# Eight subtractions of 128 columns in place of four of 256 in the edge-feature split of a graph-network kernel

## The reference, cut to what matters

```
w_ij  = silu(edge_attr_64 @ rad_w0 + rad_b0) @ rad_w1 + rad_b1
w_ij += silu(edge_attr_32 @ sph_w0 + sph_b0) @ sph_w1 + sph_b1      # 256 hidden units each
alpha = (q[receiver] * w_ij * k[sender]).sum over 16 channels of each of 8 heads / 4 * cutoff
out   = segment_sum(alpha * v[sender], receiver) / 16
```

## Time and profile before

| | us |
|---|---|
| median of 3 runs | 1711.28 (1710.13 to 1714.37) |
| span of the profiled execution | 1705.9 |
| PE busy | 1540.7 (90%) |
| DVE busy | 1368.0 (80%), 3810 instructions |
| POOL busy | 1208.1 (71%), of which L781 796.9 and L791 351.6 |
| ACT busy | 954.1 (56%) |

### The profile page before, as it was taken

How to read it: one execution, slowest core, us unless ns; L and a number is a source line. 1 busy time by engine, 2 the same in 40 slices (tenths; PEclk the granted TensorE clock), 3 DMA queues, 4 the chain that set the end, 5 groups by cost and what they waited for, 6 DMA issues and landing times.

```text
span 1705.9 us, 44927 instructions
## 1 busy us (share of the span) xinstructions
PE 1540.7 (90%) x12636; PEld 1423.3 (83%) x12636; DVE 1368.0 (80%) x3810; ACT 954.1 (56%) x1412; POOL 1208.1 (71%) x1201
## 2 busy tenths in 40 slices
PE   4389898989899876999999999999999999999995
PEld 3268787878788865999999999889999899999985
DVE  9988677777779365888888888888888888888887
ACT  3245545555565565666666655556565556555654
POOL 5577777766767327777777777777777777777772
PEclk9999999999999986999999999999999999999998
DMA  3133333333333157676666666666666666666774
GB/s 121 39 97 116 102 101 101 99 106 95 105 103 113 38 162 193 185 190 189 181 184 181 182 184 179 179 188 183 179 180 178 181 182 187 180 179 180 184 193 119
DMA packets 176696, 256.68 MB, mean 150 GB/s; under 512 B 80278, under 2 KB 91213, under 8 KB 176476
## 3 DMA queue, kind: packets, MB, share of 16 engines
q0 software_dynamic: 50240, 129.44, 28.2%
q1 hardware_dynamic: 123100, 124.61, 25.9%
q10 hardware_dynamic: 3264, 1.64, 0.3%
HBM read 232.76 MB, written 22.79 MB: 150 GB/s over the span
## 4 chain that ended last, share of the span: by engine, by line
PE 40%; POOL 30%; issue 13%; DVE 7%; ACT 4%; DMA 1%; DVEq 1%; POOLq 1%; SPq 1%; ACTq 0%
POOL arena L781 27%; PE bank L1079 19%; PE bank L1087 7%; PE bank L1061 5%; PE bank L1117 3%; POOL arena L791 3%; PE bank L1063 2%; DVE arena L1317 2%; ACT count L925 2%; PE bank L1109 2%; PE bank L1212 1%; DVE count L1486 1%; ACT nodes L943 1%; DVEq L1454 1%; DVE xsplit L1448 1%
## 5 line engine op out<-in xcount | busy, mean ns | idle before, releaser
L781 POOL DMA_INDIRECT arena<-kv_d,idx x808 | 796.9, 986 | 276.6 <-issue 272.4
L1079 PEld LDWEIGHTS bank<-w,hid 128*128 128x128 f32 x6464 | 782.1, 192 | 32.1 <-issue 8.3
L1079 PE MATMUL bank<-w,hid 128*128 128x128 f32 x6464 | 790.7, 276 | 4.9 <-ACT bank L881 4.9
L897 ACT ACTIVATE hid<-bank,b 128x512 f32<-128x512 f32 x808 | 496.2, 681 | 249.4 <-PE bank L1063 237.8
L791 POOL DMA_INDIRECT arena<-xs_d,idx x358 | 351.6, 982 | 148.7 <-issue 125.3
L1061 PE MATMUL bank<-xsplit,w_hi 128*128 128x512 f32 x808 | 348.4, 442 | 49.8 <-DVE xsplit L1448 25.9
L1448 DVE TENSOR_TENSOR xsplit<-xraw,xsplit 64x256 fp32r<-64x256 f32 x808 | 287.9, 413 | 7.8 <-issue 1.2
L889 ACT ACTIVATE xsplit<-xraw 64x1024 fp32r<-64x1024 f32 x202 | 211.9, 1050 | 84.9 <-DMA xraw<-in_sph_t 71.7
L1061 PEld LDWEIGHTS bank<-xsplit,w_hi 128*128 128x128 f32 x808 | 156.8, 194 | 82.8 <-ACT hid L897 30.0
L1087 PE MATMUL bank<-onehot,late 128*128 128x126 f32 x1616 | 213.8, 280 | 5.6 <-DVE late L1702 3.6
L1087 PEld LDWEIGHTS bank<-onehot,late 128*128 128x128 f32 x1616 | 192.2, 192 | 7.8 <-DVE late L1702 5.5
(11 more groups left out here) (159 smaller groups left out, 1368.0 us busy)
## 6 DMA issues: line engine op xcount, KB each, us to landing
xraw<-in_rad_t SPq DMA_DIRECT2D x207, 128.0 KB
xraw<-in_sph_t SPq DMA_DIRECT2D x414, 64.0 KB
late<-relrow_d SPq DMA_DIRECT2D x103, 256.0 KB
w_sb<-w_d SPq DMA_DIRECT2D x52, 256.0 KB
w_d<-w_sb SPq DMA_DIRECT2D x51, 256.0 KB
arena<-kv_d,idx POOLq DMA_INDIRECT x808
arena<-xs_d,idx POOLq DMA_INDIRECT x358
qwin<-q_d SPq DMA_DIRECT2D x101, 31.5 KB
```

The lines of the kernel that those rows point to most:

```text
L781: pool.indirect_dma_start(gath[:, k, t * width:(t + 1) * width], None, table, bass.IndirectOffsetOnAxis(ap=idx[:, pair.slot(4), j * TILES ...
L897: act.activation(hid[:, s.slot(2), c, :], hid_ps[s.sub(4, c, 4 * s.total).slot(len(hid_ps))][:, :], ACT.Silu, bias=b0[:, c:c + 1]).then_in ...
L1079: mm = pe.matmul(w_ps[:, t * D:(t + 1) * D], hid[:, b, c, t * P:(t + 1) * P], w1[:, c, :], start=False, stop=(c == 3), skip_group_check=True)
```

## The change

`split_lo` forms the low part in eight subtractions of 128 columns, where it took four of 256. The columns, the operands and the signal at the end stay as they were.

```
                 for m in range(2):
-                    for half in (slice(0, GE // 2), slice(GE // 2, GE)):
-                        last = dve.tensor_tensor(xsplit[RAD:P, b, m, half], xraw[:, k, m, half],
-                                                 xsplit[0:RAD, b, m, half].bitcast(F32), ALU.subtract)
+                    for t in range(TILES):
+                        own = slice(t * P, (t + 1) * P)
+                        last = dve.tensor_tensor(xsplit[RAD:P, b, m, own], xraw[:, k, m, own],
+                                                 xsplit[0:RAD, b, m, own].bitcast(F32), ALU.subtract)
                 last.then_inc(mlp.s_lo, 1)
```

## The result

The changed kernel is slower: 1727.84 us median of 4 runs (1722.50 to 1731.29), against 1710.86 for the kernel before beside it. The ratio is 1.0099, 95% interval 1.0082 to 1.0115, so some 17 us, where 6.5 us of gain were forecast. The profiled execution took 1728.92, its span 1727.1.

The account below looks back on a forecast made before the run. Sweep 2 was taken as bound by POOL's rate of issuing gathers. Gathers -8.5, start of sweep 1 -0.4, DVE +0.5 and +1.9 gave -6.5 us, from 1711.3 to 1704.8 us, range 1701 to 1713.

Parts of the forecast that it names:

- The mechanism and its size: Sweep 2: subtractions with two SBUF inputs lock out gathers for their column time; half the columns, 8.6 us less waiting.
- forecast 1.69: DVE: a run of eight subtractions takes 1.69 us, 0.27 us more than the run of four.
- forecast 8.5, bounds 7 and 11: Sweep 2: gathers wait 8.5 us less in the subtractions; low end 7.0 by the formula, high end 11 by phase.
- half a microsecond: End of sweep 2: share of the gain from 49 of 808 gathers after 1573 us, where the chain has left POOL.
- The second case: Sweep 2: the gathers' wait doesn't shrink, the fixed costs stay, 1713.7 us; chance 0.16.
- The case of the fixed cost at its upper bound: Nine runs on the chain pay 0.8 us each, 7.2 against 8.9 gained: 1709.6 us; chance 0.13.
- What shortens the gathers shortens sweep 2: Sweep 2: PE runs 35 us behind its own pace, held by POOL, so shorter gathers gain up to 35 us.
- The test itself: Sweep 2: the wait formula summed over all DVE kinds gave 38.1 us against 31.5 measured.
- sweep 1 at +1.9 us: Sweep 1: seven subtraction runs on the chain, 0.27 us longer each, cost 1.9 us.
- a rival on code: DVE's sweep 2 loop no longer stays loaded: stalls at ten turns, 26 us added, 1731 us; chance 0.09.
- Its criterion: Sweep 2's loop body grows to 208 working instructions, close to the 228 of sweep 1's loop, which stalls each turn.
- -8.5 + 0.5: Sweep 2: 8.5 us gained on gathers' waits, 0.5 us lost by two longer runs on the chain at its ends.

Follow-up runs that it names:

- the 80 memsets: Kernel before with 80 one-element memsets between the two sweeps: 1716.48 us, 1.0046.
- eight in sweep 1: Kernel before with eight subtractions in sweep 1 alone: 1736.24 us unshifted; 1722.40 us shifted by 64 one-element memsets between the sweeps.
- eight in sweep 2: Kernel before with eight subtractions of 128 columns in sweep 2 alone, code not shifted: 1738.26 us, 1.0172.
- its shifted twin: Kernel before with eight subtractions in sweep 2 alone, plus 34 memsets ahead of sweep 1 and 30 between the sweeps: 1709.48 us, 1.0003.
- the 184 memsets: Kernel before with 184 one-element memsets between the two sweeps: 1736.59 us, 1.0156.
- the shifted kernel before: Kernel before with 34 one-element memsets ahead of sweep 1: 1706.03 us, 0.9978.
- the shifted changed kernel: Changed kernel with 16 one-element memsets ahead of sweep 1 and 100 between the sweeps: 1715.63 us, 1.0036.
- The five-piece kernel with the delay on DVE: Kernel before with a 192-column reduction ahead of each unit's four subtractions in sweep 1, 29 memsets ahead of sweep 1, 60 between the sweeps: 1712.02 us, 1.0005.
- DVE's two reductions in sweep 2: Kernel before with one unused reduction ahead of each run of four subtractions in sweep 2: 192 columns 1712.71 us, 512 columns 1712.37 us.

## Why the prediction was wrong

**The mechanism and its size were right.** The run of eight took 1.70 us (forecast 1.69), 0.203 us apart (0.2). The gathers' waits in the subtractions fell by 10.3 us (forecast 8.5, bounds 7 and 11). One small count was wrong: 81 gathers and not 49 start after 1573 us, which at this rate is 0.9 us of the gain and not half a microsecond. The second case, a wait that doesn't shrink, falls: the waits halved. The case of the fixed cost at its upper bound falls too, by 1.70 us.

**The step that failed first: "What shortens the gathers shortens sweep 2", with the other kinds left as they were.** I took the waits kind by kind, as if gathers met instructions at random, and tested this with all kinds. The test itself gave the warning: the formula had 5.9 us for L1702 with `alpha`, and the total was a fifth too high. Read from the rows, that product held gathers for 1.7 us: a fixed phase was sparing it, since nearly all its gathers came 0.38 to 0.56 us after its start. With a run 0.27 us longer and a gather let go 0.07 us sooner on average, 29 gathers came 0.06 or 0.07 us after its start. Its waits rose by 15.2 us and ate the 10.3. That is shown from three sides: the timelines, the return of these waits with eight subtractions in sweep 2 alone, and their fall to 2.5 us, with 0.82% of the time, when that product was cut.

**The second: sweep 1 at +1.9 us.** I counted seven runs on the chain, each with 0.27 us. The measured term is 4.6 us for DVE's time (some 3 us to either side by the intervals). The chain of the kernel before shows what was on the path before, not what gets onto it: after the change it holds 13 stretches of L1449 in sweep 1.

**The third: the place of the code in sweep 1 was no term at all.** The prediction had a rival on code, and took sweep 2's loop and the number of its working instructions. The cause was real and the place wrong: sweep 1's loop, already streaming, went from six pieces to seven with its head ten instructions before the end of one, while sweep 2's loop stayed in three by luck, with room for two more instructions by the count. What it said of a stall in sweep 2 was seen in other kernels: gaps of 3.0 to 3.9 us for 0.5, and 8 us (the 80 memsets), 14 (eight in sweep 1, unshifted against shifted), some 25 (eight in sweep 2: 28.8 against its shifted twin, less the 3.8 that the shift of sweep 1 gives) and 27 (the 184 memsets), against its price of 26. Its criterion (208 working instructions against 228) is wrong: the same loop of 312 instructions stalls or not by where it begins.

**The sum again**, from the ratios. Against the shifted kernel before (0.9978): DVE's time in sweep 1 +0.27% (4.6 us), sweep 2 by itself +0.25% (4.3 us), together 8.9 us; the shifted changed kernel has +0.58%, 9.9 us. Its place of the code costs the changed kernel 0.63%, 10.8 us, of which the kernel before pays 0.22%, 3.8 us, as well. 9.9 + 10.8 - 3.8 = 16.9 us. This last line comes out at the result by construction, since its three terms are differences between four ratios; each is good to 3 or 4 us. The check is 8.9 against 9.9, and it is a loose one: with 653 instructions sweep 1's loop can't lie in five pieces, so the 9.9 should hold the cost of the sixth as well. For sweep 2 the forecast was -8.5 + 0.5 = -8.0; the 12.3 us between this and +4.3 are the 12.8 us by which the alpha product's waits rose between the same two kernels (2.3 to 15.1). All waits together rose by 3.2 us there, with 4.3 in the time.

**What stays open.** What the place of the code does after a turn in sweep 1 is shown by its effect (78.1 to 79.0 us a turn with five pieces, 78.8 to 79.5 with six, 80.3 with six and the head near the end, 81.3 to 82.1 with seven), not step by step. The five-piece kernel with the delay on DVE, at 79.5, is left out of this. PE's stretches at 1.2 GHz grow with it, and no run separates the two. Whether DVE's two reductions in sweep 2 cost 3.6 us by the waits or by time wasn't parted either. Why the same stalls cost 8 us in one kernel and 25 in another is open too. That DVE has less slack in the dear ones is not it, since the kernels with 80 and with 184 memsets have the same work in their loops. The costs of 8, 14, 25 and 27 us stand in the order of PE's time at 1.2 GHz, 27, 41, 44 and 51 us; what makes the clock fall at six turns in one and at all ten in another no run shows.

## What to carry to other kernels

Waits between two engines that run in a fixed phase don't average out: before shortening one, list what the gathers (or whatever is held) will meet next, and how long the longest such instruction is. Cut the long ones first or together; here the pair gained 10 us where one half lost 4 and the other did nothing. And before believing any result that adds instructions to a loop, count where its body lies: an A/B with a few harmless instructions ahead of the loop tells the change from its place, and here the place alone was worth from 4 us of gain to 27 of loss, more than the change itself.

## What the runs showed of the hardware

- DVE's program arrives in packets of 8 KB, 128 instructions each (the only size but 129 that sorts all 18 kernels). A loop of 312 to 372 instructions that lies in three pieces of 128 is not fetched again after its first turns (14 kernels). In four pieces it is, with about five packets a turn (45 in 750 us at 83 us a turn), and DVE stands still for 3.0 to 3.9 us at each turn (four kernels). In sweep 1 the packets from 205 to 520 us are 23 with the loop in five pieces (six kernels), 26 or 27 with six (nine) and 29 or 30 with seven (three). That there is room for four pieces, one of them fetched ahead, is my inference from this, and no run shows it. The Trainium skill (Runtime: NRT & Kernel Launch, "Instruction fetch mechanics") gives 32 KiB, which agrees, refilled in blocks of 16 KiB, and a stall for a branch whose target isn't in the window of two. For this queue the runs speak against blocks of 16 KiB: its packets have 8 KB, and in pieces of 256 instructions no offset at all puts the four stalled loops over more pieces than the others. (Another queue of instructions, q8 in the same profiles, does move packets of 16 KB.)
- A product with both inputs in SBUF holds an indirect transfer on GpSimd for up to 0.50 us (128x512), 0.10 us at the same point when it is cut to 128 columns. The Trainium skill (SBUF — State Buffer, "Who interferes with whom") infers that `tensor_tensor` does not stall descriptor generation; the gather of 1.45 us speaks against it.
- The same ten stalls of DVE, 32 to 34 us in all in each of four kernels, came with 27, 41, 44 and 51 us of PE at 1.2 GHz between 700 and 1600 us, and with 8, 14, 25 and 27 us of loss. PE wasn't at 1.2 GHz there for more than 3.4 us in any kernel without them.
- Eight subtractions of 64x128 stand 0.203 us apart, four of 64x256 0.336, and four products of 128x128 0.203. A one-element memset of DVE took 0.023 us in a row of 100.
